# Entering the gated FFN of a two-layer flamingo block: one up chunk earlier, four residual tiles copied by ScalarE and added later by VectorE

## The reference, cut to what matters

```python
x = x + tanh(g_xattn[0]) * L0_xattn(ctx, ctx, layernorm(x), ...)     # long convolution
x = x + tanh(g_ffn[0])   * L0_ffn(layernorm(x), ...)                 # int8 FFN
x = x + tanh(g_xattn[1]) * L1_xattn(layernorm(x), ctx, ...)
x = x + tanh(g_ffn[1])   * L1_ffn(layernorm(x), ...)

def L1_xattn(input1, input2, ...):            # per batch, 8 batches
    p   = softmax(theta(input2) @ phi(input1))
    t_x = p @ g(input1)
    h   = relu((t_x - mean) * rsqrt(var + 1e-5) * ln_gamma + ln_beta)
    return out_w @ h + out_b + input2

def L1_ffn(x, ...):
    up1 = linear_bit(x, w1, g1); up2 = linear_bit(x, w2, g2)
    return linear_bit(silu(up1) * up2, w3, g3)

def linear_bit(x, w, g):
    xq = act_quant(rmsnorm(x, g))             # rows rounded to 8 bits
    wq = ternary_quant(w)
    return xq @ wq.T
```

## Time and profile before

| | us |
|---|---|
| median of 3 runs | 637.16 (635.78 to 637.71) |
| the profiled execution | 637.47 |
| its span in the trace | 635.7 |
| TensorE busy | 608.2 (96% of the span) |
| VectorE busy | 542.8 (85%) |
| ScalarE busy | 474.3 (75%) |
| GpSimd busy | 352.3 (55%) |

### The profile page before, as it was taken

The page is one execution under the profiler, slowest core; times in us unless marked ns, Lnnn a source line. Parts: engine busy times, 40 slices in busy tenths (PEclk is TensorE's granted clock), DMA queues, the critical chain, the costliest instruction groups (busy, mean ns, idle before and its releaser), DMA issues.

```text
span 635.7 us, 9329 instructions
## 1 busy us (share of the span) xinstructions
PE 608.2 (96%) x2775; PEld 359.6 (57%) x2804; DVE 542.8 (85%) x1066; ACT 474.3 (75%) x716; POOL 352.3 (55%) x432
## 2 busy tenths in 40 slices
PE   6899999999999999989999999999788999999996
PEld 6777777777777444444445565555333444444443
DVE  3697888889999889876779988899898999999864
ACT  3469785765764899987763487667689999999984
POOL 2589888888877454310000111114488989889861
PEclk9899999999999999999999999999999999999999
DMA  8959896799999689739359900000116666566651
GB/s 301 379 196 309 291 331 230 251 326 338 340 306 317 258 274 305 183 90 358 140 108 197 249 26 16 16 17 17 51 46 170 182 167 181 165 187 171 181 154 50
DMA packets 141989, 125.20 MB, mean 197 GB/s; under 512 B 96048, under 2 KB 104000, under 8 KB 140800
## 3 DMA queue, kind: packets, MB, share of 16 engines
q1 hardware_dynamic: 134512, 110.52, 57.4%
q10 hardware_dynamic: 7440, 14.24, 6.7%
HBM read 68.04 MB, written 33.64 MB: 160 GB/s over the span
## 4 chain that ended last, share of the span: by engine, by line
PE 67%; DVE 13%; ACT 10%; issue 5%; DMA 2%; POOL 2%; SPq 0%; ACTq 0%; DVEq 0%; POOLq 0%
PE ps L1226 22%; PE ps L1506 14%; PE ps L1522 8%; PE ps L1344 7%; ACT turn L1015 4%; PE ps L1433 3%; PE ps L1463 3%; PE ps L1481 2%; PE ps L1437 2%; PE ps L1235 2%; PE ps L1413 1%; PE ps L1423 1%; DMA arena<-kpad_d 1%; DVE turn L1899 1%; ACT arena L968 1%
## 5 line engine op out<-in xcount | busy, mean ns | idle before, releaser
L1226 PE MATMUL ps<-arena 128*128 128x288 f32 x640 | 160.8, 408 | 4.3 <-DMA arena<-kpad_d 2.8
L1226 PEld LDWEIGHTS ps<-arena 128*128 128x128 f32 x640 | 119.6, 190 | 36.2 <-issue 3.4
L1506 PE MATMUL ps<-arena 128*128 128x512 bf16 x510 | 113.4, 379 | 4.1 <-DVE arena L2094 4.0
L1506 PEld LDWEIGHTS ps<-arena 128*128 128x128 bf16 x512 | 49.5, 98 | 66.0 <-DVE arena L2094 3.2
L737 POOL TENSOR_TENSOR arena<-arena 128x512 f32<-128x512 f32 x64 | 80.3, 1275 | 8.9 <-DVE arena L2094 7.9
L621 POOL TENSOR_TENSOR arena<-arena 128x1024 f32<-128x1024 f32 x32 | 60.6, 1893 | 17.9 <-issue 11.3
L1522 PE MATMUL ps<-arena 128*128 128x512 bf16 x241 | 57.1, 379 | 1.9 <-ACT arena L1129 0.7
L1375 PE MATMUL ps<-arena 128*128 128x512 bf16 x251 | 55.3, 379 | 1.2 <-DVE arena L1843 0.9
L1344 PE MATMUL ps<-arena 128*128 128x512 bf16 (+1 forms) x249 | 55.4, 379 | 0.6 <-ACT arena L968 0.3
L628 POOL TENSOR_TENSOR turn<-turn 128x512 f32<-128x512 f32 x31 | 40.5, 1306 | 22.8 <-DVE turn L1678 22.8
L2094 DVE SCALAR_TENSOR_TENSOR arena<-ps,up_scale,arena 128x512 f32<-128x512 f32 x64 | 46.7, 745 | 5.8 <-ACT arena L1105 5.0
(11 more groups left out here) (232 smaller groups left out, 1281.0 us busy)
## 6 DMA issues: line engine op xcount, KB each, us to landing
arena<-in_L_ffn_w SPq DMA_DIRECT2D x48, 512.0 KB, 6.1
arena<-kpad_d ACTq DMA_DIRECT2D x16, 512.0 KB, 7.1
hq_d<-arena SPq DMA_DIRECT2D x14, 512.0 KB, 2.7
tern_d<-late SPq DMA_DIRECT2D x24, 256.0 KB, 5.4
arena<-in_ctx SPq DMA_DIRECT2D x4, 1024.0 KB, 11.4
arena<-in_L_ffn_w ACTq DMA_DIRECT2D x8, 512.0 KB, 5.8
arena<-in_ctx SPq DMA_DIRECT2D x2, 2048.0 KB, 10.6
x_d<-arena SPq DMA_DIRECT2D x4, 1024.0 KB, 5.3
```

The lines of the kernel that those rows point to most:

```text
L1226: last = pe.matmul(ps[:, 4 * s + lo, 0:NB * PAIRS], toep[:, u, (LB - 1 - lo + li) * P:(LB - lo + li) * P], kv[:, s, li, :], start=(li == 0 ...
L1506: last = pe.matmul(ps[:, bank, :], xq4T[:, s, 4 * j + k, :], w[:, k, c * L:(c + 1) * L], start=(k == 0), stop=(k == LB - 1))
```

## The change

Four things are changed, all at the passage.

1. TensorE makes chunk 0 of tile 0 within batch 7, between the transposes and the value product, into banks 0 and 1 instead of 3 and 5. It waits there for the weights, the transposed input and ScalarE's last projection (`th_out`) and VectorE's additions of batch 5 (`x3_done`). Chunk 1 follows the value product, then `latent_mean(7)`, `out_proj(6)`, chunks 2 and 3, `out_proj(7)`, tile 1.
2. The four tiles of batches 6 and 7 are no longer added to the residual straight from PSUM. ScalarE copies them with their bias from banks 0 and 1 to `xo`, 8 KB of each partition of `turn` (`x3_copy`), two at the head of tile 0 and two in tile 1 behind its second `silu`. VectorE adds `xo` to the residual from SBUF later (`x3_add`): two behind `h_scales` of tile 0, two behind `h_scales` of tile 2. `attn_end(6)` and `attn_end(7)` are gone.
3. ScalarE loads its table for Silu ahead of batch 7's copies of the probabilities, and does the first `silu` right behind `relu(6)`. In tile 0 the fourth `silu` stands ahead of `x_quant(2)`.
4. VectorE does `gate(0, 0, 0)` within the body of batch 6, behind `x_scales(1)`.

The diff, without the functions that are only moved:

```diff
+        xo = turn[:, L:5 * L].rearrange("p (r l) -> p r l", r=4)
...
         def up_banks(t, c):
 
+            if isinstance(t, int) and t == 0 and c == 0:
+                return 0, 1
             if isinstance(t, int) and t < 2:
                 return 3 + c % 2, 5 + c % 2
...
+                if not nxt:
+                    act.activation(junk[:, 0:1], eps_ln[:, 0:1], ACT.Silu)
                 for k in range(4):
                     act.wait_ge(S["pt_tr"], 4 * b + k + 1)
...
                 else:
                     relu(b - 1)
+                    silu(0, 0, 0)
+
+            def x3_copy(b):
+                for o in range(2):
+                    act.wait_ge(S["wt_done"], 2 * b + o + 1)
+                    act.activation(xo[:, 2 * (b - NB + 2) + o, :], ps[:, o, :], ACT.Identity,
+                                   bias=cols3[:, 2 + o:3 + o]).then_inc(S["x3_done"], 1)
...
-                silu(t, s, 0)
+                if prev:
+                    silu(t, s, 0)
                 if late and t == 1:
                     x_centre(t + 2)
+                silu(t, s, 1)
                 if not prev:
+                    x3_copy(NB - 2)
                     relu(NB - 1)
-                silu(t, s, 1)
+                if late and t == 1:
+                    x3_copy(NB - 1)
...
-                if late and t in (1, NT - 1):
+                if late and t in (0, 1, NT - 1):
                     silu(t, s, 3)
...
-            act.activation(junk[:, 0:1], eps_ln[:, 0:1], ACT.Silu)
...
                 if not nxt:
+                    pe.wait_ge(S["bw_ready"], 12)
+                    pe.wait_ge(xT_in[0], 16)
+                    pe.wait_ge(S["th_out"], NB)
+                    pe.wait_ge(S["x3_done"], 6 + 2 * NB - 4)
+                    up(0, 0, range(1))
                     pe.wait_ge(S["ln_ready"], b)
...
-                if not nxt:
-                    out_proj(b - 1, NB)
...
-                        if 4 * t + c >= 2:
+                        if 4 * t + c >= 3:
                             pe.wait_ge(S["h_done"], 4 * t + c + 1)
...
+            up(0, 0, range(1, 2))
             latent_mean(NB - 1)
-            pe.wait_ge(S["bw_ready"], 12)
-            pe.wait_ge(xT_in[0], 16)
-            up(0, 0, range(4))
+            pe.wait_ge(S["h_done"], 3)
+            out_proj(NB - 2, NB)
+            up(0, 0, range(2, 4))
+            pe.wait_ge(S["x3_done"], 6 + 2 * NB - 2)
             out_proj(NB - 1, NB)
...
                     x_scales(1, 1)
+                    gate(0, 0, 0)
                     x_stats(2)
                 if late and b == NB - 1:
-                    attn_end(b - 1)
                     latent_ln(b)
...
+            def x3_add(r):
+                x = x_res[:, NT - 4 + r, :]
+                v.wait_ge(S["x3_done"], 6 + 2 * NB - 4 + r + 1)
+                dv.done(v.tensor_tensor(x, xo[:, r, :], x, ALU.add))
+
-            gate(0, 0, 0)
+            gate(0, 0, 1)
             x_max(2)
-            gate(0, 0, 1)
...
             h_scales(0, 0)
+            x3_add(0)
+            x3_add(1)
             gate(1, 1, 1)
-            attn_end(NB - 1)
             gate(1, 1, 2)
...
             ffn_body(2, 2, True, True, False)
+            x3_add(2)
+            x3_add(3)
```

More of the change, by code:

```diff
@@ L1162, in ffn_body @@
                     x_quant(t + 2)
-                if not (late and t in (1, NT - 1)):
+                if not (late and t in (0, 1, NT - 1)):
                     silu(t, s, 3)
@@ L1508, in up @@
                         last.then_inc(S[done], 1)
+            project(0, 0)
+            scores(0, 0)
+            attn_body(0, 0, True, False)
+            with pe.Fori(0, NB // 2 - 1) as i:
+                for u in range(2):
+                    attn_body(2 * i + 1 + u, (1 + u) % 2, True, True)
+            attn_body(NB - 1, 1, False, True)
             def hidden_T(t, n, parts, bank):
```

27 lines of the change are left out of this document (10 added, 17 removed).

## The result

The changed kernel takes 641.04 us (median of 6 runs, 640.28 to 642.95), the kernel before 637.0 us on the same chip (6 runs, 635.78 to 638.8). The ratio is 1.0068, 95% interval 1.0052 to 1.0083: slower by 4.0 us. The profiled execution took 642.95 us, its span is 641.1.

The account below looks back on a forecast made before the run. It took TensorE to bound the FFN's steady part, the end being set by its entry into tiles 3 and 4. A loss of 1.9 us at tile 4 on the median 637.16 gave 639.1 us, range 635.8 to 641.4.

Parts of the forecast that it names:

- the first rival: Tile 3: tile 5's CAST also waits for GpSimd's x_gain, TensorE loses 1.9 us more: 641.0 us, chance 0.28.
- The chunk in the gap: TensorE, batch 7: a 1.73 us chunk fills a 1.46 us wait; between 0.25 us lost and 1.73 gained, only a lead.
- ScalarE's additions at nothing: ScalarE, tiles 0 and 1: four copies of 0.69 us fit into its waits, and the table load moves, at no cost.
- Additions 0 and 1 wait for the rest of the product: VectorE at 469.2 us: 0.65 us wait for x_gain(3), then 0.55 and 0.6; chunk 3 of tile 1 starts at 471.75.
- Then 0.3 us earlier into tile 3: Without attn_end(7), gate(1,3) follows at 473.55 instead of 473.92; ScalarE passes 0.3 us gained through tile 2.
- Additions 2 and 3, +1.9 us at tile 4: VectorE behind h_scales(2): held by x_gain(5), gate(3,0) is 2.13 us late; TensorE loses 1.9 us at tile 4.
- The widening of tile 5: Tile 3: GpSimd's x_gain about 0.1 us ahead holds the CAST; TensorE loses 1.9 us more, chance 0.28.
- widening not caught: Likeliest case: additions held, but tile 5's CAST does not wait for x_gain: 639.1 us, range 638.3 to 639.9, chance 0.36.
- Nothing behind it: TensorE behind the start of tile 4: no waits there, so nothing gives back the 1.9 us; no other wait expected.
- the other rivals: Additions not held, 637.3 or 639.2 us, chance 0.21; TensorE's lead of 1.73 us kept, 635.2 us, chance 0.12.
- Additions that are not held: VectorE's additions don't wait for GpSimd: -0.85 + 0.97 = +0.1 us, 637.3 us (0.17), or 639.2 with the CAST caught (0.04).
- the rule that was weighed: VectorE and GpSimd share SBUF ports as an exclusive lock, kept by whoever starts first; by it the sum is +1.9 us.

Follow-up runs that it names:

- e4: Changed kernel without ScalarE's four copies and VectorE's additions from SBUF; attn_end adds from PSUM again, batch 6 inside latent_ln(7): 637.10 us, ratio 0.9981 to 1.0005.
- e10: Changed kernel without VectorE's four additions, nothing in their place, ScalarE's four copies kept: 635.29 us, ratio 0.9957 to 0.9984.
- e7: Changed kernel plus ten filling matmuls into a free PSUM bank, ahead of chunk 3 of tile 1: 641.56 us, ratio 1.0047 to 1.0083.
- e8: Changed kernel with the edits of e1, e3 and e7 together: 638.56 us, ratio 1.0008 to 1.0032.
- e1: Changed kernel with the two late additions replaced by bn_stats of the same length with one SBUF input: 641.32 us, ratio 1.0053 to 1.0088.
- e2: Changed kernel with all four additions replaced by bn_stats of the same length with one SBUF input: 640.12 us, ratio 1.0029 to 1.0061.
- e5: Kernel before plus two additions of two SBUF operands into unused scratch, behind h_scales of tile 2: 639.92 us, ratio 1.0036 to 1.0077.
- e3: Changed kernel with x_widen's CAST moved ahead of the second maximum, from tile 2 on: 640.24 us, ratio 1.0024 to 1.0062.
- e12: Changed kernel, batch 7 added from PSUM; of batch 6's copied tiles VectorE adds one behind tile 1's CAST, GpSimd the other: 636.61 us, ratio 0.9977 to 1.0005.
- e11: Changed kernel, batch 7 added from PSUM by VectorE, batch 6's copied tiles added by GpSimd in its idle time: 636.17 us, ratio 0.9973 to 1.0003.

## Why the prediction came out as it did

The time, 641.04 us, lies in the range, 1.9 us above the forecast of 639.1 and on the number of the first rival, 641.0 us. The rival's two losses happened as it says, but that its number is met to 0.04 us is luck: its sum has 3.8 us of loss, the trace has 4.70, and the medians differ by 4.0. Step by step:

- *The chunk in the gap.* It was to be a lead only, and it was: e4 has 0.5 us of it left, e10 0.9. The list of TensorE's waits for VectorE left out the two of tile 2, 1.95 us ahead of it and 0.96 us inside, which are longer than two of the three it names.
- *ScalarE's additions at nothing.* The copies took 0.69 us each. With them and without the additions (e10) TensorE is 0.4 us further ahead at tile 3 than with additions from PSUM and no copies (e4), so they cost nothing that shows.
- *Additions 0 and 1 wait for the rest of the product.* They were to start at 469.2 us, behind an `h_scales(0)` that ends 0.95 us earlier, and start at 469.27 (469.99 less the 0.72 us of the alignment). For their length, predicted 0.65 + 0.55 + 0.6 = 1.8 us, measured 1.80. Chunk 3 of tile 1 was to start at 471.75 us; it did at 471.79, aligned in the same way.
- *Then 0.3 us earlier into tile 3.* This term was mis-sized: +0.74 us instead of -0.3. The step took the chunk behind the wait at 1.73 us. It took 2.86, and tile 2's 32 matmuls ran through 8.90 us, part of them at a granted clock of 0.50, behind a wait that had grown to 2.56 us. With the wait filled (e7, e8) tile 3 is at -0.05 and -0.04: 0.8 us of the error of 1.0 are the clock, and the other 0.25 is most of the gain that was to reach ScalarE. In e7 `gate(1,3)` comes only 0.11 us earlier than before (475.69 less the 1.88 of its alignment, against 473.92), not 0.37.
- *Additions 2 and 3, +1.9 us at tile 4.* Measured +1.93. The additions took 2.86 us, the rest of the product (1.71) and 1.15. e1 splits it: 0.9 for the wait, 1.0 for two more instructions on an engine without idle time there. The waits named by the rows are 1.37 and 0.22 us; the rest is that each breaks the overlap of 0.17 us between one group of matmuls and the next.
- *The widening of tile 5.* The forecast gave this 0.28 and left it out; it happened. Its working held: GpSimd was ahead by 0.16 us (0.1 worked out), the CAST waited 2.05 us (2.2), TensorE lost 1.68 (1.9). The failed step is the likeliest case, "widening not caught". It rested on a lead of 0.1 us either way, and what decided it showed in five kernels, after, e1, e2, e5 and e7: as soon as VectorE has two instructions more in tile 3, its CAST falls behind `x_gain`. Only e3 and e8, where it stands ahead of the second maximum, escape.
- *Nothing behind it.* Nearly: +0.35 us at tile 6 was not priced. It goes with the CAST (absent in e3 and e8).

One sum of the other rivals is off without consequence: 1.2 us less the slack of 0.26 is 0.94 and not 0.97. Additions that are not held were run in e2, and the step to tile 4 is +1.01 there.

For the additions and the CAST beside `x_gain` the rows and the runs bear out the rule that was weighed, by which whoever starts first keeps the shared ports for its whole instruction. By the Trainium skill ("SBUF — State Buffer", section "SBUF: two separate sides") the lock concerns a VectorE instruction with two SBUF inputs, or in a two-port mode, against GpSimd's. The trace agrees on both sides of it: 2.26 us for an addition beside `x_gain` and 0.68 for one input in the same place (e1) or for two inputs with no product beside them (e12). The CAST has one input, so by that rule it could only be the mode that makes it wait, and no run shows its mode. That the first keeps the ports does not hold in the rows for a small instruction: with GpSimd's L746 0.11 us ahead of the CAST neither was held (0.56 and 0.42 us), and with L746 0.02 us ahead it was L746 that took longer, 0.84 us. The long `x_gain`, ahead by 0.16 to 0.17 us, held the CAST in each of the five kernels.

What stays open: whether the fall of the clock adds to the median of the whole kernel, whether e11 beats before, and what costs the moved CAST its 0.25 to 0.41 us at tile 8.

## What to carry to other kernels

Before moving an operand from PSUM to SBUF, look at what GpSimd runs at that moment: the same addition costs 0.68 us alone and up to 2.26 beside a long GpSimd product. A lead on one engine is worth only what the engine that releases it can keep up with, and two instructions more on an engine without idle time can flip a race of 0.1 us a tile later, at a price of 2 us. When two kernels differ by less than 1%, compare runs with equal granted clock, and align the traces at a common instruction ahead of the change; but look in the trace where the clock was low, since a mean of 0.994 came from the passage in after's profiled execution and one of 0.995 from the first 30 us in e7's.
